# Three kinds of DMA move to the SP queue: the q stores, the output stores and the residual loads of an attention and expert-FFN layer on eight cores

## What is computed

```python
qkv = jnp.einsum('bsd,de->bse', x, W_qkv)
q, k, v = jnp.split(qkv, 3, axis=-1)            # 16 heads of 128
attn = jnp.einsum('bhqd,bhkd->bhqk', q, k) / math.sqrt(HEAD_DIM)
attn = attn + alibi_bias(seq_len, N_HEADS)[None] + causal_mask(seq_len)[None, None]
y = jnp.einsum('bhqk,bhkd->bhqd', jax.nn.softmax(attn, axis=-1), v)
x = _layernorm(x + y @ W_o)
...
base = x @ W.T + bias
delta = jnp.einsum('ner,eor->no', (x A^T) * coeff, B)   # coeff: softmax of the top 2 of 16 experts
x = _layernorm(x + base + delta)
```

## Time and profile before

| what | us |
|---|---|
| median of 4 runs | 5322.05 |
| the four runs | 5018.77, 5625.33, 5745.75, 5000.77 |
| the profiled execution | 5046.58 |
| its span on the slowest core (core 7) | 5045.0 |
| spans of the 8 cores | 4969.5 to 5045.0 |
| attention's first q load, on core 7 and on core 4 | 864.35 and 797.49 |
| SP issues the 16 loads (8 MB) of the second `kv_gen`, core 7 | 830.89 to 856.57 |
| landing of a q store, median of the page | 2.5 |

### The profile page before, as it was taken

How to read it: one execution, slowest core, us unless ns; L and a number is a source line. 1 busy time by engine, 2 the same in 40 slices (tenths; PEclk the granted TensorE clock), 3 DMA queues, 4 the chain that set the end, 5 groups by cost and what they waited for, 6 DMA issues and landing times.

```text
span 5045.0 us, 39200 instructions; the slowest of 8 cores (4969.5 to 5045.0 us)
## 1 busy us (share of the span) xinstructions
PE 4339.6 (86%) x15336; PEld 2978.7 (59%) x15336; DVE 785.4 (16%) x1312; ACT 357.4 (7%) x595; POOL 46.4 (1%) x88
## 2 busy tenths in 40 slices
PE   8888799998998997998989989986999845888882
PEld 6676687686785785876767857843443324333330
DVE  0000000212112102112112121031000142111115
ACT  0000000101101001001011010021000000000000
POOL 0000000000000000000000000000000000000000
PEclk8777899999999998999999999988999967999996
DMA  5122224224232232232232232224111101000001
GB/s 159 56 59 73 84 75 146 80 70 127 79 106 82 81 115 93 73 119 72 88 119 76 93 107 80 67 72 124 50 40 50 29 21 34 25 25 25 25 17 67
DMA packets 373492, 376.47 MB, mean 75 GB/s; under 512 B 18624, under 2 KB 336192, under 8 KB 373056
## 3 DMA queue, kind: packets, MB, share of 16 engines
q1 hardware_dynamic: 322048, 256.51, 16.7%
q10 hardware_dynamic: 43776, 92.29, 6.1%
q0 software_dynamic: 7488, 25.17, 1.3%
HBM read 348.75 MB, written 25.17 MB: 74 GB/s over the span
## 4 chain that ended last, share of the span: by engine, by line
PE 78%; DMA 9%; DVE 9%; issue 2%; SPq 1%; ACT 0%; DVEq 0%; ACTq 0%; POOL 0%; POOLq 0%
PE bank L290 18%; PE bank L314 18%; PE bank L514 10%; PE bank L954 9%; PE bank L678 9%; DMA posb<-alibid 6%; PE bank L407 3%; PE bank L355 3%; PE bank L364 3%; DVE st_sb L439 2%; DMA qh<-wqkv 1%; SPq L108 1%; PE bank L869 1%; DVE st_sb L459 1%; PE bank L969 1%
## 5 line engine op out<-in xcount | busy, mean ns | idle before, releaser
L290 PE MATMUL bank<-xb,wk 128*128 128x256 f32 x4096 | 914.1, 384 | 0.0
L314 PE MATMUL bank<-wv,xb 128*128 128x256 f32 x4096 | 909.0, 383 | 0.0
L290 PEld LDWEIGHTS bank<-xb,wk 128*128 128x128 f32 x4096 | 790.6, 193 | 122.5 <-issue 9.7
L314 PEld LDWEIGHTS bank<-wv,xb 128*128 128x128 f32 x4096 | 785.0, 192 | 117.3 <-issue 6.7
L678 PE MATMUL bank<-yfm_all,wocol 128*128 128x512 f32 x1024 | 448.9, 596 | 32.1 <-DMA yfm_all<-y_hbm 32.1
L954 PE MATMUL bank<-x1fm,wtcol 128*128 128x512 f32 x1024 | 452.0, 600 | 12.1 <-DMA bP_sb<-bP 12.1
L355 PE MATMUL bank<-pt_sb,V 128*128 128x512 f32 (+3 forms) x768 | 333.6, 517 | 105.6 <-ACT pt_sb L447 105.2
L407 PE MATMUL bank<-qh,K 128*128 128x512 f32 (+3 forms) x768 | 331.4, 542 | 99.4 <-DMA qh<-q_hbm 67.8
L678 PEld LDWEIGHTS bank<-yfm_all,wocol 128*128 128x128 f32 x1024 | 195.5, 191 | 279.8 <-issue 279.8
L954 PEld LDWEIGHTS bank<-x1fm,wtcol 128*128 128x128 f32 x1024 | 199.2, 195 | 267.3 <-issue 267.3
L364 PE MATMUL bank<-pt_sb,ones_sb 128*128 128x512 f32 (+3 forms) x768 | 321.7, 502 | 0.0
(11 more groups left out here) (83 smaller groups left out, 1643.0 us busy)
## 6 DMA issues: line engine op xcount, KB each, us to landing
xb<-xT SPq DMA_DIRECT2D x256, 512.0 KB, 7.0
qh<-wqkv SPq DMA_DIRECT2D x64, 256.0 KB, 6.3
wk<-wqkv SPq DMA_DIRECT2D x32, 512.0 KB, 10.6
posb<-wqkv SPq DMA_DIRECT2D x64, 256.0 KB, 4.4
wv<-wqkv SPq DMA_DIRECT2D x32, 512.0 KB, 8.6
posb<-alibid ACTq DMA_DIRECT2D x32, 512.0 KB, 4.1
wocol<-wo SPq DMA_DIRECT2D x64, 256.0 KB, 4.9
wtcol<-wT SPq DMA_DIRECT2D x64, 256.0 KB, 3.8
```

The lines of the kernel that those rows point to most:

```text
L290: mmk = p.op("tensor", (lambda bi_, fc_, oc_, tb_, par_: (lambda e: e.matmul(banks[bi_][:, 0:256], wk_sb[par_][:, fc_ * 256 + oc_ * 128: f ...
L314: mmk = p.op("tensor", (lambda bi_, fc_, tt_, tb_, par_: (lambda e: e.matmul(banks[bi_][:, 0:256], xb[tb_ % 2][:, fc_ * 256 + tt_ * 128: f ...
```

## The change

`store` gets a parameter for the queue. The 64 stores of q and the 4 stores of the result now ask for SP ("sync") instead of GpSimd, with the same waits ahead of them. The two `xos` buffers now belong to SP, so the 32 residual loads, and the waits for the buffers' last use, stand on SP instead of ACT. The 16 stores of y stay on GpSimd. Nothing else is changed.

```diff
-    def store(self, dst, src, deps=()):
+    def store(self, dst, src, deps=(), qeng="gpsimd"):
         if self.stsem is None:
             self.stsem = self._mksem("s")
-        self.p.waits("gpsimd", deps)
-        mk = self.p.op("gpsimd", (lambda d_, s_: (lambda e: e.dma_start(
+        self.p.waits(qeng, deps)
+        mk = self.p.op(qeng, (lambda d_, s_: (lambda e: e.dma_start(
             out=d_, in_=s_)))(dst, src), self.stsem, 16)
...
                         qob.store(dap(q_hbm, oc * 128 * OWN + qp * 512 + qq * 256,
                                       [[OWN, 128], [1, 256]]),
-                                  st_sb[qq][:, ob * 128: ob * 128 + 256], deps=[emk])
+                                  st_sb[qq][:, ob * 128: ob * 128 + 256],
+                                  deps=[emk], qeng="sync")
...
-                xosb = [B("scalar"), B("scalar")]
+                xosb = [B("sync"), B("sync")]
...
                     mk = x2buf.store(
...
-                        deps=[apmks[(q4 * 4 + 4) * 2 - 1]])
+                        deps=[apmks[(q4 * 4 + 4) * 2 - 1]], qeng="sync")
```

## The result

The changed kernel takes 5240.6 us (median of 7 runs); the kernel before, in the ten runs now at hand, 5015.3. The ratio is 1.0368, with a 95% interval of 1.0319 to 1.0417: 3.7% slower, about 185 us. So the 185 is the ratio's 3.68% of 5015, and not the difference of the two medians.

What follows compares the result with a forecast made beforehand. The prediction took TensorE to bound the kernel, holding 78% of the chain of waits. Its terms, 125 + 35 + 13 + 0 - 1 = +172 on the profiled 5046.6, gave 5219 us, range 5105 to 5480.

Steps and rivals of the forecast that it cites:

- TensorE's clock behind a gap: Query stage: TensorE restarts at a lower clock after each of 25 gaps, 1.4 each, 35 us, bounds 12 and 64.
- The gaps: Query stage: next block's weights wait behind q stores; 17 gaps of 4.5 and 8 of 5.55, 125 us, bounds 101 and 206.
- The six late boundaries: Query-stage boundaries where an xb load already holds SP: two store issues add 0.74 each, 4.4 us in all.
- The way into attention: Query stage's end to attention's first head: 3 us gained, 16 lost to 8 MB of loads; +13, bounds -3 and +25.
- The residual loads: On SP behind the yfm_all loads, then ahead of the next block's weights: covered, cost 0, upper bound 46 us.
- The result's stores: Kernel's end: SP follows the last add after 0.15 instead of 0.56, with a shorter issue; -1 us, bounds 0 and -2.
- the prediction's own sign of being wrong: Wrong if new waits were under 3 us or over 7, query stage unchanged, or output projection or tail moved over 5.
- The first q load: Sign in the profile after: attention's first q load comes 125 to 165 us later.
- The rival through the clock: Query stage: gaps keep TensorE's load low, no core is held down, 66 us come back; 5091 to 5153, chance 0.12.
- The long gaps: Query-stage boundaries: loads land at the stage's median of 6.3, so gaps are longer; 307 us, some 5350, chance 0.13.
- the harmless queue: SP's order would not matter, store waits being over in time; only the end's 1 to 3 us gained, 5044, chance 0.05.
- theory H: Stated for a follow-up kernel: the program's end goes with GpSimd's number of stores; 1.7 us there, ratio 0.980 to 0.984.

Runs made afterwards that it cites:

- second experiment: Kernel before with the residual loads and output stores on SP, the q stores still on GpSimd; ratio 0.996 to the kernel before.
- the first experiment: Kernel before with only the 64 q stores moved to SP, residual loads and output stores left where they were; ratio 1.035 to the kernel before.
- The last kernel of the table: Kernel before with the xb load deferred one generator step, q stores on ACT and output stores on SP; ratio 0.9814 to the kernel before.

## Why the prediction was right or wrong

The prediction's text forecast +172 us on the profiled execution, 3.4%; measured are 3.68%, or 185 us. The direction of its sum and the cause stood. Two steps failed: the base on which the time stands, and the size of the clock's term.

The first is the step from the sum to the time, "The profiled execution took 5046.6, so 5219". The only figure that a reader had for the kernel before was the median of four runs, 5322, and against it 5219 is a gain of 2%, the reverse of what the text argues: the costs were added to one base and stand against another. The runs showed 1.0368, slower, over a kernel before that takes 5015 and not 5322. A forecast should name the ratio next to the time. The base was off the other way too: the profiled execution had two cores that reached attention some 65 late, and it lay above the comparable runs of 4982 to 5035. That the time came out 0.4% below the 5240.6 measured is luck: against the comparable 5190 to 5207 it is too high, since a base some 40 too high outweighs a sum some 12 too low.

The second is the term for TensorE's clock behind a gap, 35 in the sum and 56 measured. Its lower anchor, 0.46 for a wait of 2.67, divides 7.4 us by 16 waits, but TensorE has only 7 waits in that window of the trace before (core 7, 4637 to 4784):

```profile
PE bank L998 <- DVE x2fm L989: 18.6, 7, 2.7
```

By these it is 1.05 a wait, and the middle of 1.05 and 2.6 would have been 1.8 a gap, or 46 for the 25. Term by term:

- *The gaps, 125.* Measured 120.4 of added waits on cores 0 to 3, with 25 new ones at the 25 boundaries named. On core 0 they are 4.2 to 4.8 at 14 of the 17 boundaries without a chunk (the others 5.4, 5.7 and, the first of all, 6.2) and 5.4 to 5.5 at seven of the eight with one (the other 6.2). The terms of the 4.5 were right too, with two small errors that cancel: VectorE's end to SP's issue took 0.04 and not 0.15, and between the end of the store's issue and that of the load lay 0.10 that the sum does not have; landing and wake-up, 3.23, are the 3.2 forecast with the store's 0.2. The six late boundaries were to cost 4.4 more; on core 0 their waits and that of the start are 3.3 shorter.
- *TensorE's clock behind a gap, 35.* This is the term that failed in size: 56 measured, 2.2 a gap in place of 1.4. "A gap of 4.5 to 5.6 lies between these; I take 1.4" went near the middle of a misread 0.46 and 2.6. The runs show besides that a gap of 4.3 already costs nearly what one of 12 does: the sets of eight behind it go at half the pace, and core 0 lags by 2.2 a new gap and by 2.3 to 2.5 behind the six longer ones. The rule of the Trainium skill that was set beside it (TensorE: Matmul & The Clock Gate, HAM oscillation — how this bites in real kernels) would have paid every gap in full, and here the trace agrees with it: on core 0 the first group lasted 2.8 to 3.75 behind every one of the new waits, where 1.89 is normal. Waits of 0.9 did not do it.
- *The way into attention, +13.* The +16 for the first head measured +14.0, with 11 from the 8 MB alone. The -3 belongs to the query stage: from the last q store's issue to the first q load it took 4.4 before and 2.3 after, -2.1. Together +12.
- *The residual loads, 0.* Right.
- *The result's stores, -1.* The store follows VectorE by 0.07 instead of 0.56, as worked out, and from its issue to the end the kernels that differ in these four stores differ by 1.1 (second experiment against before) and 1.3 (changed kernel against the first experiment). But the end is 6.4 us shorter in all. The other 5 come with the q stores; that was not foreseen and is told below. It also passes the prediction's own sign of being wrong, a tail that moves by more than 5.
- *The first q load, 125 to 165 us later.* It came 176.4 later on cores 0 to 3, for the clock's sake.
- *The rival through the clock (5091 to 5153).* The gaps do not keep the clock up. In the profile after, all of cores 4 to 7 had 0.83 between 24 and 440 us, against 0.88 to 0.89 on cores 0 to 3, and reached attention at 987 to 995, 21 behind the others; the first experiment shows the same on four cores. But they lost less than cores 6 and 7 before, which had 0.77 to 0.78 and came 65 late. So in these two executions the query stage of core 7 grew by 122 only, and the slowest span by 143. Whether the gaps shorten the lowered stretch, or it is just shorter in some executions, is not shown.
- *The long gaps (5350)* and *the harmless queue (5044)* did not happen. The Trainium skill's advice to put simple stores on the Sync queue (DMA: Bandwidth & Descriptors, Issuing engine by pattern) holds for the queue alone: on SP landing fell from 2.5 to 1.9 us and the issue from 0.54 to 0.34; on ACT landing was 2.8, the issue 0.33, and the query stage lost nothing. It says nothing of what stands behind the store.

## What to carry to other kernels

A queue that runs ahead with loads must hold nothing that waits for the present step. A store that waits for the step's result turns every later load on that queue into a load that is issued too late; put it on a queue with nothing urgent behind it, or write it behind as many of the next step's loads as cover its wait. In this kernel a new gap on TensorE of 4 us or more cost the gap plus some 2 us of slow restart. Look for the same pattern in the loads that are there already: here moving the `xb` loads by one step was worth 1.8%.

## What was not expected

The end of the program goes with the number of stores that GpSimd issued. In the kernel before, the last output store of core 0 is issued at 4979.14 and lands 7.0 later, at 4986.1, but the span goes on to 4993.7, for another 7.5 us in which no engine and no DMA shows work. After the change it is 5155.94, 6.5 and 5164.1: 1.7 us. The last store and the span of core 0, before (timeline, then the row of the cores' spans):

```profile
4979.14 0.74 POOL L118 DMA_DIRECT2D out<-x2fm  x1 [11.99 <-DVE x2fm L1031]
```

```profile
core 0: 4993.7 us, clock 0.927
```

and after:

```profile
5155.94 0.37 SPq L118 DMA_DIRECT2D out<-x2fm  x1
```

```profile
core 0: 5164.1 us, clock 0.920
```

From the issue of the last store to the end it takes 14.6 to 14.8 with 84 stores on GpSimd, 13.5 with 80, 9.4 to 9.7 with 20 and 8.2 to 8.5 with 16, whether SP or ACT took the q stores. In the steps from 84 to 80 and from 20 to 16 the last store itself changes its queue, and lands some 0.4 sooner. Between 20 and 84 only the q stores move, and that is 0.08 us for each. The last kernel of the table was built for this: with 16 left on GpSimd, 1.6 to 1.7 us follow the landing of its last store on cores 0 to 3, as theory H has it. What runs in that time the profile does not show, and it stays open. It explains 5 us of the 43 by which the q stores on ACT seemed faster; with the 3 of the other two stages that is 8, and the interval of the ratio begins at 18. So the stages do not explain that ratio. The fastest runs of the two kernels, 4982.6 and 4971.1, lie only 11.5 apart; where the rest of the 43 comes from stays open.
